# Moving the zero fill of the expert rows into the front, and a three-set ring in the edge count

## The chip, the cores and the metric

One Trainium2 chip, one of its cores. The time is device microseconds of one execution; the kernel before was timed three times.

## What is computed

One program chains four blocks on 1250 nodes with 512 features and 20000 edges sorted by receiver:

```python
x = x + graph_attention(layernorm(x), src, dst)      # softmax over edges, 8 heads
x = x + expert_ffn_top2(layernorm(x))                # 8 experts, capacity
x = x + tensor_product_messages(layernorm(x), edges) # MLP on edges, segment sum
x = x + expert_banks_top1(layernorm(x))              # two banks of 8 experts
```

The change touches the first one alone, and scratch memory that the second and the fourth use. The attention of the first block is done densely. Each pair (sender, receiver) gets the number of edges between them, and the logarithm of that number is added to the dense scores; a pair without an edge gets a very negative value. So three stages come first: the **front** (records of the edges are sorted into tiles of 128 edges, and queries, keys and values are computed), the **count** (the table of logarithms), and the attention itself.

## The kernel before, in words

Each stage is a block: its engines run their own programs, and all engines meet at its end, so a stage lasts as long as its slowest engine or queue.

**Front** (`front`, L137). The SP queue loads indices, attributes, x and the three weight matrices (L217), and later stores the queries to `q_dram` in eight transfers (L221), two for each of four groups of columns, each pair behind the evictions that fill the buffer QT (L219). ACT may refill QT for groups 2 and 3 only when the stores of groups 0 and 1 have landed. GpSimd (POOL) scatters the edge records: 157 indirect DMAs from `recs` to `rec_dram` (L266), one per column of 128 edges. They go in batches of 16, and batch b waits until all of batch b-2 have landed, so 16 to 32 are under way. VectorE (DVE) computes their positions, normalises x and computes tables: `low`, `turnI`, `spotI` and `endI` say for each tile of edges which block of receivers it belongs to, where its sums lie in PSUM and when a block is complete.

**Count** (`count_edges`, L561). The records come back as `recs_in`, in two parts. There are 176 tiles of 128 edges, worked in 44 sets of four. For a set DVE makes one `ohD` (L655: 4 one-hots of the receiver, 128 wide, all in one instruction) and four `ohS` (L659: the one-hot of half the sender's number, 625 columns used, WIDEN = 632 written). TensorE (PE) multiplies them: two matmuls a tile (512 and 113 columns, L677) add the counts into one of four regions of PSUM. ACT takes the logarithm of a finished block (L696) and clears its region (L701). The ring of one-hots holds CRING = 8 tiles, which is AHEAD = 2 sets: DVE waits before set g until PE has finished set g-2 (semaphore `counted`). PE reads the four PSUM offsets of a set from SBUF into registers with one TENSOR_LOAD (L670) ahead of the set; POOL reads a register for every set too (L620) and grants DVE the set when its region is free. The keys of the one-hots are computed by `keys` (L636 to L643) for the first 32 tiles at the start, and for the other 144 between sets 7 and 8.

In this stage the SP queue loads the records (L602) and the first queries (L545), and then calls `fill_zeros` (L606 to L609) for three arrays in DRAM: xin0 (4004 rows), xin_sp and xin_fq (2176 rows each), 512 floats a row, in pieces of 128 rows: 66 transfers. They stay zero until expert stages much later scatter rows into them. The stage's end waits for them.

At the end of its grants POOL splits the first tile of queries (L552, L554) for the attention.

Of the kernel before, what the change touches and what calls it, by code (L numbers as in the profile page):

```python
# [7 lines left out]
F16 = mybir.dt.float16  # L8
# [3 lines left out]
ALU = mybir.AluOpType  # L12
# [6 lines left out]
TILES = NODES // P  # L19
# [2 lines left out]


LANES, EPP = 128, 1
HALFB, BLOCKS, REGIONS, REGION, CRING = 64, 2 * TILES, 4, 1024, 8
EMAIN = EDGES // LANES
ETAIL = EDGES - EMAIN * LANES
ECOLS = EMAIN + 1
# [3 lines left out]
GROUPS = (EDGES + BLOCKS * GROUP) // GROUP  # L32
GROUPS += GROUPS % 2
ETILES = GROUPS * EPP
SLOTS = ETILES * LANES
assert GROUPS % 4 == 0 and CRING == 8
EHID = 64
ECHUNKS = -(-ETILES // 8)
REC = 16
# [16 lines left out]
BANKS = ("sp", "fq")  # L56
# [16 lines left out]
def gnn_moe_gnn_moe(nc, I, out):  # L73
# [17 lines left out]
    def sems_in(stack):  # L91

        def allocate(*names):
            handles = [nc.alloc_semaphore(name=fresh(n)) for n in names]
            stack.callback(finished.extend, handles)
            return handles
        return allocate
# [22 lines left out]
    with top:  # L120
        sb = tile_in(top)
# [15 lines left out]
        def front(KT, V, turnI, spotI, endI):  # L137

            with ExitStack() as st:
# [9 lines left out]
                done, moved, upper_moved, v_moved = sems_in(st)(  # L149
                    "product_done", "product_moved", "upper_moved", "values_moved")  # L150
                q_stored = sems_in(st)("queries_stored0", "queries_stored1")

                srcI, dstI = sb("srcI", [LANES, ECOLS], I32), sb("dstI", [LANES, ECOLS], I32)
                a4, a8 = sb("a4", [LANES, ECOLS, 4]), sb("a8", [LANES, ECOLS, 8])
# [42 lines left out]
                with nc.Block() as block:  # L197
                    @block.sync
                    def _(sp):
                        sp.dma_start(dstI[:, 0:EMAIN], main_part(I["dst"])).then_inc(dst_in, 16)  # L200
                        sp.wait_ge(blanked, 1)
                        sp.dma_start(dstI[0:ETAIL, EMAIN:], I["dst"][EMAIN * LANES:].rearrange("(p c) -> p c", c=1)).then_inc(dst_in, 16)
                        sp.dma_start(srcI[:, 0:EMAIN], main_part(I["src"])).then_inc(src_in, 16)
                        sp.dma_start(srcI[0:ETAIL, EMAIN:], I["src"][EMAIN * LANES:].rearrange("(p c) -> p c", c=1)).then_inc(src_in, 16)
                        sp.wait_ge(fill_ready, 1)
                        whole = rec_dram.rearrange("(p c) w -> p c w", p=LANES)
                        part = ETILES // FILLS
                        for f in range(FILLS):
                            sp.dma_start(whole[:, part * f:part * (f + 1), :], fill[:]).then_inc(filled, 16)
                        for tile, name in ((a4, "edge_attr_4"), (a8, "edge_attr_8")):  # L210
                            sp.dma_start(tile[:, 0:EMAIN, :], main_rows(I[name])).then_inc(attr_in, 16)
                            sp.dma_start(tile[0:ETAIL, EMAIN, :], I[name][EMAIN * LANES:, :]).then_inc(attr_in, 16)
                        x_rows = I["x"].rearrange("(t p) d -> p t d", p=P)
                        sp.dma_start(X[0:120], x_rows[0:120]).then_inc(x_in, 16)
                        sp.dma_start(X[120:P], x_rows[120:P]).then_inc(x_in, 16)
                        for i, name in enumerate(("L0_gnn_Wq", "L0_gnn_Wk", "L0_gnn_Wv")):
                            sp.dma_start(W[i][:], I[name].rearrange("(k p) n -> p k n", p=128)).then_inc(w_in[i], 16)  # L217
                        for j in range(KC):
                            sp.wait_ge(moved, (j + 1) * len(CHUNKS))  # L219
                            for half in range(2):  # L220
                                sp.dma_start(q_dram[:, 2 * j + half, :], QT[DK * half:DK * (half + 1), j % 2, :]).then_inc(q_stored[j % 2], 16)  # L221
                        for b in range(2):
                            sp.wait_ge(q_stored[b], 16 * KC)

                    @block.gpsimd
                    def _(pool):
# [334 lines left out]
        def count_edges(LA, stage, split, turnI, spotI, endI):  # L561

            HALFN = NODES // 2
            WIDEN = 632
            PARTS = [(0, 512), (512, HALFN - 512)]
            SET = 4
            AHEAD, SETS = CRING // SET, GROUPS // SET
            EARLY_ROUNDS = 4
            with ExitStack() as st:
# [1 line left out]
                RECS = sb("recs_in", [128, ETILES, REC])  # L571
                PARTS_OF_RECS = ((0, SET * AHEAD * EARLY_ROUNDS), (SET * AHEAD * EARLY_ROUNDS, ETILES))
                loaded = sems_in(st)("recs_loaded0", "recs_loaded1")
                numbered, cleared, steps, hot, counted, logged, evicted, zeroed, tick = sems_in(st)(
                    "nodes_numbered", "cleared", "steps", "one_hots_ready", "counted", "logged",
                    "evicted", "zeroed", "tick")
                (granted,) = sems_in(st)("region_granted")
                nodes16 = sb("nodes16", [128, WIDEN], F16)
                srcI, parityI = sb("srcI", [128, ETILES], I32), sb("parityI", [128, ETILES], I32)
                halfS, local, key16 = sb("halfS", [128, ETILES]), sb("local", [128, ETILES]), sb("key16", [128, GROUPS, EPP], F16)  # L580
                ohS, ohD = sb("ohS", [128, CRING, WIDEN], F16), sb("ohD", [128, CRING // SET, 2 * HALFB, SET], F16)
                keys_by_tile = sb("keys_by_tile", [128, 2 * HALFB, SET], F16)
                least = sb("least", [128, 1])
# [14 lines left out]
                with nc.Block() as block:  # L598
                    @block.sync
                    def _(sp):  # L600
                        for part, (c0, c1) in enumerate(PARTS_OF_RECS):
                            sp.dma_start(RECS[:, c0:c1, :], rec_dram.rearrange("(p c) w -> p c w", p=128)[:, c0:c1, :]  # L602
                                         ).then_inc(loaded[part], 16)
                        sp.wait_ge(loaded[1], 16)
                        stage(sp, 0)
                        zeros_in = fill_zeros(sp, xin0, zeroed)  # L606
                        for bank in BANKS:
                            zeros_in += fill_zeros(sp, xin1[bank], zeroed)
                        sp.wait_ge(zeroed, zeros_in)  # L609

                    @block.gpsimd
                    def _(pool):
# [14 lines left out]
                    @block.vector  # L627
                    def _(dve):
                        step = Chain(dve, steps)
                        nc.vector.memset(ps[:], 0.0).then_inc(cleared, 1)  # L630

                        def keys(part):
                            c0, c1 = PARTS_OF_RECS[part]
                            mine, groups_of = slice(c0, c1), slice(c0 // EPP, c1 // EPP)
                            dve.wait_ge(loaded[part], 16)
                            nc.vector.tensor_tensor(local[:, mine].rearrange("p (g t) -> p g t", t=EPP),  # L636
                                                    RECS[:, mine, 1].rearrange("p (g t) -> p g t", t=EPP),
                                                    low[:, groups_of].unsqueeze(2).to_broadcast([128, (c1 - c0) // EPP, EPP]), ALU.subtract)
                            step(nc.vector.tensor_copy(srcI[:, mine], RECS[:, mine, 0]))
                            nc.vector.tensor_scalar(parityI[:, mine], srcI[:, mine], 1, None, ALU.bitwise_and)  # L640
                            step(nc.vector.tensor_scalar(srcI[:, mine], srcI[:, mine], 1, None, ALU.arith_shift_right))
                            nc.vector.tensor_copy(halfS[:, mine], srcI[:, mine])
                            step(nc.vector.scalar_tensor_tensor(out=key16[:, groups_of, :].rearrange("p g t -> p (g t)"),  # L643
                                                                in0=parityI[:, mine], scalar=float(HALFB), in1=local[:, mine],
                                                                op0=ALU.mult, op1=ALU.add))

                        keys(0)
                        dve.wait_ge(numbered, 1)

                        def one_hots(g, k):  # L650
                            n = SET * g
                            dve.wait_ge(granted, g + 1)
                            dve.sem_inc(tick, 1)
                            dve.wait_ge(counted, n + SET)
                            nc.vector.tensor_tensor(ohD[:, k], keys_by_tile[:],  # L655
                                                    key16[:, bass.ds(n, SET), :].rearrange("p a t -> p (a t)")
                                                    .unsqueeze(1).to_broadcast([128, 2 * HALFB, SET]), ALU.is_equal)
                            for t in range(SET):
                                last = nc.vector.tensor_scalar(ohS[:, SET * k + t, :], nodes16[:], halfS[:, bass.ds(n + t, 1)],  # L659
                                                               None, ALU.is_equal)  # L660
                            last.then_inc(hot, 1)

                        groups(dve, one_hots, lambda: keys(1))
# [2109 lines left out]
```

## Time and profile before

| | us |
|---|---|
| median of 3 runs | 1884.42 |
| lowest, highest | 1881.56, 1887.0 |
| the profiled execution | 1887.7 |
| its span, first to last instruction | 1886.1 |

The profiled execution stands 3.3 us above the median of the runs, and 1.6 us of it lie outside its span. Mean granted TensorE clock 0.926. Over the span PE is busy 84%, DVE 51%, ACT 37%, POOL 30%. Such shares are averages over stages with different limits: what the change is worth has to be read in the front (0 to 233 us) and the count (233 to 325 us).

### The profile page before, as it was taken

What the parts mean: (1) busy time and instruction counts of PE and PEld (TensorE: products, weight loads), DVE (VectorE), ACT (ScalarE), POOL (GpSimd) and SP (SyncE); (2) the same over time, 40 slices, a digit from 0 to 9 for tenths busy, and PEclk for the clock granted to TensorE, in tenths of its full rate; (3) what the DMA queues carried; (4) which work ended last, traced back from release to release, by engine and by line L of the source; (5) the groups of instructions that cost most, each with busy time, mean ns of one, the idle gap of its engine ahead of it and who ended that gap; (6) DMA issues with size and microseconds to landing.
All of it is one profiled execution on the core that took longest, in us unless ns stands there. A gap on an engine that the chain in (4) does not pass through costs nothing. (4 is left out here: it accounts for less than half of the span.)

```text
span 1886.1 us, 31693 instructions
## 1 busy us (share of the span) xinstructions
PE 1592.0 (84%) x9860; PEld 1167.2 (62%) x9860; DVE 962.2 (51%) x1950; ACT 701.8 (37%) x1610; POOL 558.7 (30%) x638
## 2 busy tenths in 40 slices
PE   0993067999999797797999999848999999898994
PEld 0551034888888555555999999844555555655662
DVE  8320088677667287351000000068999999542233
ACT  1220045555555233443221111154555555431331
POOL 6777600110110032152000000045555555133133
PEclk6997589999999899798999999969999999998997
DMA  6200091110100510547556652075555555618985
GB/s 178 61 7 6 16 354 53 23 23 12 22 11 1 124 37 1 214 135 243 211 207 232 242 196 98 17 206 170 154 155 160 156 155 149 214 44 283 340 271 181
DMA packets 131144, 252.87 MB, mean 134 GB/s; under 512 B 35345, under 2 KB 52597, under 8 KB 126573
## 3 DMA queue, kind: packets, MB, share of 16 engines
q1 hardware_dynamic: 91692, 171.81, 27.5%
q0 software_dynamic: 39360, 79.86, 15.0%
q8 instruction: 55, 0.90, 0.2%
q14 instruction: 37, 0.30, 0.1%
HBM read 196.03 MB, written 55.52 MB: 133 GB/s over the span
## 5 line engine op out<-in xcount | busy, mean ns | idle before, releaser
L1998 PE MATMUL acc<-prod,ohy 128*64 128x256 f32 x1056 | 248.5, 385 | 7.8 <-DVE prod L2116 7.8
L2042 ACT ACTIVATE ohy<-oh,RECS 128x64 f32<-128x64 f32 x704 | 187.0, 336 | 151.4 <-PE acc L1998 151.4
L1998 PEld LDWEIGHTS acc<-prod,ohy 128*64 128x64 f32 x1056 | 138.3, 137 | 132.3 <-issue 70.6
L1975 POOL DMA_INDIRECT rows<-up_dram,idx x176 | 167.4, 951 | 143.0 <-DVE prod L2116 101.6
L266 POOL DMA_INDIRECT rec_dram<-recs,pos x157 | 160.2, 1021 | 59.6 <-issue 48.9
L2001 PE MATMUL acc<-prod,ohy 128*64 128x256 f32 x704 | 177.1, 394 | 0.0
L1752 DVE TENSOR_SCALAR FT<-y_ps,b2T 128x188 f32<-128x188 f32 x32 | 13.2, 414 | 319.8 <-PE y_ps L1701 319.8
L1689 PE MATMUL hid_ps<-FT,W 128*128 128x188 f32 x1024 | 168.0, 326 | 0.7 <-ACT FT L1726 0.7
L2116 DVE TENSOR_TENSOR prod<-w_ps,rows 128x768 f32<-128x768 f32 x176 | 166.3, 945 | 0.0
L1689 PEld LDWEIGHTS hid_ps<-FT,W 128*128 128x128 f32 x1024 | 165.6, 192 | 0.9 <-issue 0.9
L1701 PE MATMUL y_ps<-hid,W 128*128 128x188 f32 x1024 | 164.5, 323 | 0.0
L1701 PEld LDWEIGHTS y_ps<-hid,W 128*128 128x128 f32 x1024 | 162.9, 190 | 0.0
L842 DVE CUSTOM_DVE_ANT_0 S<-score_ps,LA 125x1250 f32<-125x1250 f32 x80 | 116.7, 1459 | 77.4 <-PE score_ps L758 76.5
L903 ACT ACTIVATE S<-S,mx 125x1250 f32<-125x1250 f32 x80 | 107.3, 1341 | 116.2 <-DVE mx L847 116.2
L677 PE MATMUL ps<-ohS,ohD 128*128 128x512 f16 x352 | 60.3, 320 | 106.1 <-DVE ohS L659 100.1
L2061 DVE TENSOR_TENSOR MSG<-MSG,acc 128x512 f32 x178 | 120.7, 678 | 3.5 <-PE acc L1998 0.5
L677 PEld LDWEIGHTS ps<-ohS,ohD 128*128 128x128 f16 x352 | 38.7, 117 | 128.3 <-issue 123.1
L758 PE MATMUL score_ps<-KT,QS 128*125 128x512 f32 (+1 forms) x480 | 113.1, 371 | 4.0 <-PEq L598 2.1
L767 PE MATMUL turn_ps<-ident,S 125*125 125x125 f32 x800 | 108.4, 283 | 1.2 <-ACT PT L908 1.1
L776 PE MATMUL out_ps<-PT,V 125*64 125x125 f32 x1600 | 103.0, 274 | 1.5
L1637 POOL DMA_DIRECT2D yout<-ye x7 | 11.8, 1692 | 307.4 <-DVE ye L1757 307.4
L767 PEld LDWEIGHTS turn_ps<-ident,S 125*125 125x125 f32 x800 | 94.4, 190 | 12.9 <-issue 11.2
(380 smaller groups left out, 2632.4 us busy)
## 6 DMA issues: line engine op xcount, KB each, us to landing
W<-in_L_ffn_w SPq DMA_DIRECT2D x16, 4096.0 KB, 16.7
bankW_sp<-in_L_ffn_W_sp SPq DMA_DIRECT2D x2, 4096.0 KB, 23.8
xin<-zeros SPq DMA_DIRECT2D x31, 256.0 KB
h_dram<-h3e SPq DMA_DIRECT2D x22, 256.0 KB, 4.5
h<-h_dram SPq DMA_DIRECT2D x22, 256.0 KB, 2.7
QF<-q_dram SPq DMA_DIRECT2D x20, 250.0 KB, 4.3
xin_sp<-zeros SPq DMA_DIRECT2D x17, 256.0 KB
xin_fq<-zeros SPq DMA_DIRECT2D x17, 256.0 KB
```

Source lines behind the costliest of these rows:

```text
L266: pool.indirect_dma_start(out=rec_dram, out_offset=bass.IndirectOffsetOnAxis(ap=pos[0:rows_of, c:c + 1], axis=0), in_=recs[0:rows_of, c, : ...
L758: last = nc.tensor.matmul(score_ps[:P, c0:c0 + cn], QS[par][:, part, h, 0:P], KT[:, h, c0:c0 + cn], start=part == 0, stop=part == 1)
L767: last = nc.tensor.transpose(turn_ps[:P, 128 * s:128 * s + P], S[:, h % 2, P * s:P * (s + 1)], ident[:P, :P])
L842: nc.vector.tensor_tensor_reduce(out=S[:, h % 2, :], in0=score_ps[:P, 0:NODES], in1=LA[:, 2 * pairs - 2 + par, :], scale=1.0, scalar=-3e38 ...
L1689: last = nc.tensor.matmul(hid_ps[:, m % 4, 0:ROWS0], W1[b][:, k, 128 * m:128 * (m + 1)], xT[:, k, :], start=k == 0, stop=k == KC - 1)
L1701: last = nc.tensor.matmul(y_ps[:, d % 2, 0:ROWS0], W2[b][:, m, 128 * d:128 * (d + 1)], hid[:, m, :], start=m == 0, stop=m == MC0 - 1)
L1975: pool.indirect_dma_start(out=rows[:, t, :], out_offset=None, in_=up_dram, in_offset=bass.IndirectOffsetOnAxis(ap=idx[:, par, t:t + 1], ax ...
L1998: upper = lambda m: nc.tensor.matmul(acc[0:HALFB, bank, :].rearrange("p (b c) -> p b c", c=MUL)[:, m:4:3 - m, :], ohs[:, 1 + m, :], pr[:, ...
L2001: lower = lambda q: nc.tensor.matmul(acc[HALFB:128, bank, 256 * q:256 * (q + 1)], ohs[:, 0, :], pr[:, 0:3:2, :] if q == 0 else pr[:, 3:5, ...
L2042: last = nc.scalar.activation(ohy[:, t % OHY, i, :], oh[:, par, t, :], ACT.Copy, scale=RECS[:, bass.ds(BATCH * g + t, 1), 4 + i])
L2061: nc.vector.tensor_tensor(sums, sums, acc[:, bank, :], ALU.add).then_inc(taken, 1)
L2116: nc.vector.tensor_tensor(pr[:, 2:8, :].rearrange("p (a m) c -> p a m c", a=2), w[:, 2:4, :].unsqueeze(2).to_broadcast([128, 2, 3, MUL]), ...
```

## The change

The 66 transfers of zeros go to the SP program of the front: behind the loads of the weights, ahead of the stores of the queries; the front's end waits for them in place of the count's. The ring of one-hots grows from 8 to 12 tiles (AHEAD 2 to 3). With it the first part of the records becomes 48 tiles, not 32 (the second 128, not 144), the loops over sets are unrolled three times, not twice, and two sets stand behind the loop. `endI` follows CRING. To make room, WIDEN becomes 626, and `halfS` and `local` go: both are written in place over columns 0 and 1 of the records (16 floats apart), and `ohS` reads its scalar there.

```diff
-HALFB, BLOCKS, REGIONS, REGION, CRING = 64, 2 * TILES, 4, 1024, 8
+HALFB, BLOCKS, REGIONS, REGION, CRING = 64, 2 * TILES, 4, 1024, 12
...
                             sp.dma_start(W[i][:], I[name].rearrange("(k p) n -> p k n", p=128)).then_inc(w_in[i], 16)
+                        sp.wait_ge(consts, 1)
+                        zeros_in = fill_zeros(sp, xin0, zeroed)
+                        for bank in BANKS:
+                            zeros_in += fill_zeros(sp, xin1[bank], zeroed)
                         for j in range(KC):
                             sp.wait_ge(moved, (j + 1) * len(CHUNKS))
...
                         for b in range(2):
                             sp.wait_ge(q_stored[b], 16 * KC)
+                        sp.wait_ge(zeroed, zeros_in)
...
-            WIDEN = 632
+            WIDEN = 626
...
-                halfS, local, key16 = sb("halfS", [128, ETILES]), sb("local", [128, ETILES]), sb("key16", [128, GROUPS, EPP], F16)
+                key16 = sb("key16", [128, GROUPS, EPP], F16)
...
                         sp.wait_ge(loaded[1], 16)
                         stage(sp, 0)
-                        zeros_in = fill_zeros(sp, xin0, zeroed)
-                        for bank in BANKS:
-                            zeros_in += fill_zeros(sp, xin1[bank], zeroed)
-                        sp.wait_ge(zeroed, zeros_in)
...
-                            nc.vector.tensor_tensor(local[:, mine].rearrange("p (g t) -> p g t", t=EPP),
-                                                    RECS[:, mine, 1].rearrange("p (g t) -> p g t", t=EPP),
-                                                    low[:, groups_of].unsqueeze(2).to_broadcast([128, (c1 - c0) // EPP, EPP]), ALU.subtract)
+                            nc.vector.tensor_tensor(RECS[:, mine, 1], RECS[:, mine, 1], low[:, groups_of], ALU.subtract)
...
-                            nc.vector.tensor_copy(halfS[:, mine], srcI[:, mine])
+                            nc.vector.tensor_copy(RECS[:, mine, 0], srcI[:, mine])
...
-                                last = nc.vector.tensor_scalar(ohS[:, SET * k + t, :], nodes16[:], halfS[:, bass.ds(n + t, 1)],
+                                last = nc.vector.tensor_scalar(ohS[:, SET * k + t, :], nodes16[:], RECS[:, bass.ds(n + t, 1), 0],
```

The helper that it calls:

```python
        def fill_zeros(sp, target, zeroed):
            starts = range(0, target.shape[0], 128)
            for r in starts:
                m = min(128, target.shape[0] - r)
                sp.dma_start(target[r:r + m, :], zeros[:m, :]).then_inc(zeroed, 16)
            return 16 * len(starts)
```

## Rows read from the trace of the kernel before

**Rows 1.** Table of stretches: front after PE's start, its tail, the flood, the quiet.

```profile
core 0: us, PE busy (x) PEld busy (x) DVE busy (x) ACT busy (x) POOL busy (x), PEclk, DMA share, GB/s
60.00:150.00 90.00, 90.00 (x246) 46.22 (x245) 16.32 (x33) 22.23 (x43) 68.46 (x71) 1.00 0.16 35
150.00:228.00 78.00, 6.68 (x16) 2.63 (x14) 0.00 (x0) 1.64 (x3) 58.02 (x61) 0.57 0.04 6
264.00:286.00 22.00, 14.59 (x94) 10.07 (x92) 18.58 (x59) 13.54 (x18) 0.00 (x0) 1.00 1.02 378
289.00:308.00 19.00, 15.22 (x99) 10.58 (x98) 18.87 (x61) 13.52 (x17) 0.00 (x0) 1.00 0.00 1
```

**Rows 2.** Timeline of the SP queue: start, length of issue, line, transfer.

```profile
15.09 4.68 SPq L217 DMA_DIRECT2D Wqkv<-in_L_gnn_Wv  x1
64.02 26.28 SPq L221 DMA_DIRECT2D q_dram<-QT  x8
240.57 22.44 SPq L1536 DMA_DIRECT2D xin<-zeros  x32
274.49 12.34 SPq L1536 DMA_DIRECT2D xin_fq<-zeros  x17
```

**Rows 3.** The SP queue's own wait at the end of the count.

```profile
SPq L598 <- DMA xin_fq<-zeros: 3.0, 1, 3.0
```

**Rows 4.** POOL's scatter L266: the whole front, then 60 to 100 us.

```profile
L266 POOL DMA_INDIRECT rec_dram<-recs,pos x157: 869/967/4703, 18.5 to 226.8; - x157
L266 POOL DMA_INDIRECT rec_dram<-recs,pos x32: 963/967/970, 60.2 to 99.6; - x32
```

**Rows 5.** A stretch in which query stores load the DMA engines during the scatter.

```profile
82.00:84.00 2.00, 2.00 (x6) 0.88 (x5) 0.00 (x0) 0.15 (x1) 1.70 (x2) 1.00 0.95 197
```

**Rows 6.** POOL's ten scatters L2570 late in the kernel, while bank weights load.

```profile
DMA to landing us min/median/max: 8.0/9.3/11.6
```

**Rows 7.** TENSOR_LOAD L670 (ns min/median/max): 264 to 286 us, then 289 to 312.

```profile
L670 PEldq TENSOR_LOAD <-spotI x12: 625/930/1077, 264.5 to 285.8; - x12
L670 PEldq TENSOR_LOAD <-spotI x14: 328/332/335, 289.4 to 309.7; - x14
```

**Rows 8.** Waits from 215 to 345 us: us in total, times, longest.

```profile
DVE ohD L655 <- PE ps L677: 8.4, 17, 1.4
```

**Rows 9.** Timeline of DVE in the count: first set, keys, quiet sets, collision, last set.

```profile
238.88 0.42 DVE L655 TENSOR_TENSOR ohD<-keys_by_tile,key 128x512 f16<-128x512 f16 x1 [0.54 <-POOLq L622]
239.23 1.26 DVE L659 TENSOR_SCALAR ohS<-nodes,halfS 128x632 f16<-128x632 f16 x4
240.40 0.41 DVE L655 TENSOR_TENSOR ohD<-keys_by_tile,key 128x512 f16<-128x512 f16 x1
...
253.58 0.39 DVE L636 TENSOR_TENSOR local<-recs_in,low 128x144 f32<-128x144 f32 x1
...
255.57 0.42 DVE L655 TENSOR_TENSOR ohD<-keys_by_tile,key 128x512 f16<-128x512 f16 x1 [0.52 <-DVE key L643]
...
289.86 0.42 DVE L655 TENSOR_TENSOR ohD<-keys_by_tile,key 128x512 f16<-128x512 f16 x1
...
307.11 0.42 DVE L655 TENSOR_TENSOR ohD<-keys_by_tile,key 128x512 f16<-128x512 f16 x1
...
312.84 0.41 DVE L655 TENSOR_TENSOR ohD<-keys_by_tile,key 128x512 f16<-128x512 f16 x1
...
320.11 0.43 DVE L655 TENSOR_TENSOR ohD<-keys_by_tile,key 128x512 f16<-128x512 f16 x1
```

**Rows 10.** Timeline of PE and POOL at the collision.

```profile
309.68 2.18 POOL L554 TENSOR_TENSOR QS<-QF,QS 128x1000 fp32r<-128x1000 f32 x1
...
313.06 5.18 PE L677 MATMUL ps<-ohS,ohD 128*128 128x512 f16 x24 [2.97 <-DVE ohS L659]
```

**Rows 11.** The shortest DVE TENSOR_SCALAR, one column: busy us, mean ns.

```profile
L886 DVE TENSOR_SCALAR has<-mx 125x1 f32<-125x1 f32 x10 | 1.0, 102 | 0.0
```

**Rows 12.** Timeline of DVE in the front: the twenty 157-column one-hots.

```profile
4.55 3.19 DVE L286 TENSOR_SCALAR ge<-dst 128x157 f16<-128x157 f16 x20
```

More of the change, by code:

```diff
@@ L35 @@
 SLOTS = ETILES * LANES
-assert GROUPS % 4 == 0 and CRING == 8
+assert GROUPS % 4 == 0 and CRING % 4 == 0
 EHID = 64
@@ L151, in front @@
                 q_stored = sems_in(st)("queries_stored0", "queries_stored1")
+                (zeroed,) = sems_in(st)("rows_zeroed")
                 srcI, dstI = sb("srcI", [LANES, ECOLS], I32), sb("dstI", [LANES, ECOLS], I32)
@@ L573, in count_edges @@
                 loaded = sems_in(st)("recs_loaded0", "recs_loaded1")
-                numbered, cleared, steps, hot, counted, logged, evicted, zeroed, tick = sems_in(st)(
+                numbered, cleared, steps, hot, counted, logged, evicted, tick = sems_in(st)(
                     "nodes_numbered", "cleared", "steps", "one_hots_ready", "counted", "logged",
-                    "evicted", "zeroed", "tick")
+                    "evicted", "tick")
                 (granted,) = sems_in(st)("region_granted")
@@ L641, in keys @@
                             step(nc.vector.tensor_scalar(srcI[:, mine], srcI[:, mine], 1, None, ALU.arith_shift_right))
-                            nc.vector.tensor_copy(halfS[:, mine], srcI[:, mine])
+                            nc.vector.tensor_copy(RECS[:, mine, 0], srcI[:, mine])
                             step(nc.vector.scalar_tensor_tensor(out=key16[:, groups_of, :].rearrange("p g t -> p (g t)"),
-                                                                in0=parityI[:, mine], scalar=float(HALFB), in1=local[:, mine],
+                                                                in0=parityI[:, mine], scalar=float(HALFB), in1=RECS[:, mine, 1],
                                                                 op0=ALU.mult, op1=ALU.add))
```

## The prediction, on record before the changed kernel ran

> **What bounds the kernel now.** I read the table of stretches first, then the SP queue's timeline, then the groups and waits inside the count.
>
> The front ends with POOL, not with PE, DVE or the DMA engines. From 150 to 228 us PE is busy 6.7 of 78 us and DVE not at all, while POOL works through its scatters at a DMA share of 0.04 [rows 1]. The 157 scatters start between 18.5 and 226.8 us, one every 1.27 us in steady state: (226.8 - 60.2) / 131 for the last ones [rows 4]. So the DMA engines have room there, and whatever else is put in the front costs nothing as long as the scatters keep their pace.
>
> The count has two faces. From 289 to 308 us DVE is busy 18.87 of 19 us and bounds the stage: 11 sets between the `ohD` at 289.86 and the one at 307.11, which is 1.568 us a set [rows 1, 9]. From 264 to 286 us, while zeros fill the DMA engines (share 1.02, 378 GB/s), DVE is busy only 18.58 of 22 us and waits for PE, though PE is busy just 14.59 us [rows 1]. What holds PE is its register read: the TENSOR_LOAD ahead of each set takes 930 ns in the flood (median) and 332 ns without it [rows 7]. The matmuls of a set last 1.24 us (14.59 us for 94, eight a set [rows 1]), and the load can't overlap most of them, so a set takes PE 22 / 11.75 = 1.87 us there, above DVE's 1.57. DVE's waits for PE add up to 8.4 us [rows 8]. The zeros are issued from 240.57 to 286.83 us (46.3 us for 66 transfers) and the last lands some 3 us later [rows 2, 3]; the stage goes on past 320, so their own end holds nobody.
>
> **The change, part by part.** The sum is made on DVE's stream of sets, since its last `ohD` (320.11) sets the end of the count in both kernels.
>
> Before: first `ohD` 238.88, last 320.11, that is 81.2 us for 43 steps [rows 9].
>
> After, with no wait for PE: 43 x 1.568 = 67.4 us. To this come the second part of the keys, 255.57 - 253.58 = 2.0 us, and the collision with POOL's split of the queries: from 307.11 to 312.84 DVE needed 5.73 us for two sets that otherwise take 3.14, so 2.6 us [rows 9, 10]. The split follows POOL's last grants and so stays a few sets ahead of the end; I keep the 2.6. The sum is 72.0 us, 9.2 less than before. The wait row gives nearly the same from the other side: 8.4 us [rows 8].
>
> That all of the waits go, not only those of the flood, rests on the ring. Three PE sets at the low clock took 5.18 us after the collision, 1.73 a set against DVE's 1.57 [rows 10]; with three sets in the ring DVE runs through such a stretch. The ring alone would do little against the flood, because there PE's rate, not its latency, is short.
>
> Small terms. The loop over sets is unrolled thrice. The step from 238.88 to 240.40 holds no turn of the loop and takes 1.52 us, the mean of quiet steps is 1.568 with a turn in every second, so a turn costs about 0.1 us [rows 9]; 22 turns become about 15, -0.6 us (bounds 0 and -0.7). WIDEN 632 to 626: 6 columns at 0.28 ns (worked out below) by 176 are -0.3 us. The in-place keys write every sixteenth float: two copies, each bounded by the strided subtraction's 0.39 us [rows 9]; I take +0.3 us. Part 0 of the records grows from 256 to 384 KB and loads while DVE clears PSUM; if that cover fell short it would be by less than 1 us. The second part of the keys now comes after set 11, at the same cost. DVE's extra run-ahead costs no PSUM, since grants are as before; POOL's and ACT's register reads get shorter too, off the path. Together -0.6.
>
> In the front SP is free for zeros from 19.8 us [rows 2]; they share the engines with x and the weights, which are ahead of them in the same queue, and need their 46 us after that, so they flow until about 80 us. Past them are moved the stores of the queries, first issued at 64.02: they come up to 15 us late, and ACT's refill of QT a few us late. PE and ACT have that slack many times over: PE's work ends before 160 us, the stage near 230. The scatters: during the flood some 35 of them are issued. The nearest rows say that their issue does not care. From 60 to 100 us, while the query stores run, 32 scatters take 963/967/970 ns, and in 82 to 84 us the share is 0.95 [rows 4, 5]. Their landing may be late: under weight loads ten scatters landed after 8 to 11.6 us [rows 6]; but a batch waits for records issued at least 16 x 1.27 = 20 us earlier, so this is hidden, with 9 us to spare. Cost of the move: 0, bounds 0 and +14 to +25 (the rival below). A gain has no ground there, since the scatters run at their pace already.
>
> The Trainium skill has a rule against this: "DMA: Bandwidth & Descriptors", queues, rings and completion order, says each DMA engine round-robins between queue rows and drains a whole packet, of some 9 to 17 descriptors, before it switches. By it each scatter would stand behind packets of zeros; no row here shows packets in such a mix. At worst this lengthens the landings above.
>
> Sum: -9.2 - 0.6 = -9.8 us; the wait row would make it -9.0. I take **-9.5**. On the profiled execution: span 1886.1 to 1876.6, time 1887.7 to 1878.2. The median of the runs stands 3.3 lower: 1884.4 to **1874.9**.
>
> **The rivals.**
>
> *The scatter slows (slower side).* Place: L266 during the flood, 35 to 80 us. POOL also reads its positions from SBUF, as PE reads its offsets, and the flood made that read longer by 0.6 us [rows 7]. If each scatter took 0.6 us more, a pace of 1.87 would lose 45 x (1 - 1.27/1.87) = 14 us; if its 0.967 us grew by the same factor, 930/332 = 2.8, the pace would be 3.0 and the loss 26 us. Against -9.5 this gives +5 to +16: 1889 to 1901, most likely 1893. It decides from a loss of 9.5 us, a mean DMA_INDIRECT above 1.31 us in the flood. For it: nothing here shows a scatter against writes of zeros from SBUF at 380 GB/s. Against it: 970 ns at most under the stores [rows 4], which also go from SBUF to DRAM. Chance 8%.
>
> *The narrow one-hot loses its rate (slower side).* Place: L659, 176 times. 626 columns split in two halves of 313, an odd number, and the second half no longer begins on a 4-byte boundary. The 632-column form comes every (240.40 - 239.23) / 4 = 0.293 us [rows 9]. The 157-column one of the front takes 3.19 / 20 = 0.160 [rows 12]; the difference is 0.28 ns a column, with a fixed 0.116 us, near the 0.102 of a one-column instruction [rows 11]. So 157, odd in length and in its halves' start, runs at the rate of 632. If 626 did run at half that rate, it would cost 626 x 0.28 = 0.175 us more by 176, 31 us, for a net +21: 1906. Chance 4%. The Trainium skill speaks on both sides: "VectorE: DVE Perf Modes", mode 2×_1P, asks for 4-byte alignment; "Vector Engine (DVE) Microarchitecture Reference", section 5.1, says that alignment makes no difference, and the 157-column one-hots [rows 12] agree with the latter.
>
> *PE's clock takes part of it back.* With the waits gone PE still idles 0.3 us a set, and it starts the stage cold. At the low level three sets took 5.18 us [rows 10]. If about half of the 44 sets ran so, PE would bound them at 1.73 to 1.95, and the gain would lose 22 x 0.16 to 0.38 = 3.5 to 8 us: a gain of 1.5 to 6, 1878.5 to 1883. Against it: from 289 to 308 us, at just this load, the clock stayed at 1.00 [rows 1]. Chance 16%.
>
> *More than the sum.* DVE, three sets ahead, loses less in the collision, or the split slides behind the last set: 2.6 us more, and PE's cold start is absorbed too: -12 to -13, 1872. Chance 10%.
>
> **How the numbers follow.** The forecast (gain 7 to 11.5, 1873 to 1877.5) has 62%. About 0.3%, 5.6 us, is what a measurement of this kernel can tell from no change. Faster by more: 62 + 10 and a part of the clock's case, 76%. Within: the rest of the clock's case and the gentler end of the scatter's, 14%. Slower: 10%. The range reaches from the "more" case to the clock's case, with a us for the spread of medians: 1870 to 1881.5.
>
> **What would show it.** TENSOR_LOAD L670 near 330 ns throughout; DVE's wait for PE under 1.5 us; count from first to last `ohD` near 71.5 us; `ohS` at 0.29 us a piece; scatters in 35 to 80 us at 0.97 and the last one starting at 226.8 as before; zeros issued from about 20 to 77 us. Wrong it would be if the front's last scatter moves, if `ohS` takes 0.47, or if PE runs at 0.5 clock in the middle of the count.

## The result, and the profile after

| | before | changed |
|---|---|---|
| median of 6 runs, us | 1884.07 | 1871.24 |
| lowest, highest | 1881.56, 1887.0 | 1868.04, 1875.17 |
| ratio, 95% interval | | 0.9936 [0.9917, 0.9954] |
| span of the profiled execution | 1886.1 | 1873.4 |

The change gained 12.8 us in the medians, 12.7 in the spans; 9.5 were forecast. A second series (e0 below) gave 0.9947 [0.9927, 0.9966].

**The count.** First and last `ohD`, and the quiet and flooded stretches of before [rows 1, 9], now (timeline of DVE, then the table of stretches):

```profile
239.54 0.42 DVE L655 TENSOR_TENSOR ohD<-keys_by_tile,key 128x512 f16<-128x512 f16 x1 [0.54 <-DVE key L643]
...
241.05 0.42 DVE L655 TENSOR_TENSOR ohD<-keys_by_tile,key 128x512 f16<-128x512 f16 x1
...
299.13 0.41 DVE L655 TENSOR_TENSOR ohD<-keys_by_tile,key 128x512 f16<-128x512 f16 x1
299.47 3.94 DVE L659 TENSOR_SCALAR ohS<-nodes,recs_in 128x626 f16<-128x626 f16 x4
303.33 0.41 DVE L655 TENSOR_TENSOR ohD<-keys_by_tile,key 128x512 f16<-128x512 f16 x1
...
309.36 0.41 DVE L655 TENSOR_TENSOR ohD<-keys_by_tile,key 128x512 f16<-128x512 f16 x1
```

```profile
core 0: us, PE busy (x) PEld busy (x) DVE busy (x) ACT busy (x) POOL busy (x), PEclk, DMA share, GB/s
264.00:286.00 22.00, 18.70 (x117) 12.63 (x116) 22.00 (x74) 17.56 (x23) 0.00 (x0) 1.00 0.00 1
```

From the first one-hot to the last it takes 69.8 us, not 81.2, so 11.4 us are gained. DVE is busy 22.00 of 22 us, and nearly every step from one `ohD` to the next is 1.51 us. Its waits for PE (8.4 us [rows 8]) are gone from the table of waits; what is left of idle time before `ohD` is 1.1 us behind its own keys. The steps that are longer are two at PE's cold start (1.71 and 1.57 us), the one with the second keys and the one at the collision. The collision with POOL's split still costs 4.20 - 1.51 = 2.7 us. The register reads of PE stay short, but for the first one (531 ns at 238.1 us), over all 44 sets (min/median/max ns, against 625/930/1077 in [rows 7]):

```profile
L670 PEldq TENSOR_LOAD <-spotI x44: 327/331/531, 238.1 to 310.6; - x44
```

**The front.** SP's timeline, POOL's scatter over the whole front and from 20 to 80 us, its landing from 20 to 80 us, and a stretch of the table:

```profile
19.29 35.31 SPq L1536 DMA_DIRECT2D xin<-zeros  x32
54.64 12.86 SPq L1536 DMA_DIRECT2D xin_sp<-zeros  x17
67.54 13.31 SPq L1536 DMA_DIRECT2D xin_fq<-zeros  x17
80.90 10.74 SPq L226 DMA_DIRECT2D q_dram<-QT  x8
```

```profile
L272 POOL DMA_INDIRECT rec_dram<-recs,pos x157: 873/968/4706, 18.9 to 227.4; - x157
L272 POOL DMA_INDIRECT rec_dram<-recs,pos x42: 963/970/4706, 18.9 to 79.6; - x42
DMA to landing us min/median/max: 3.0/4.8/10.2
```

```profile
64.00:80.00 16.00, 16.00 (x46) 8.29 (x45) 0.00 (x0) 1.92 (x4) 12.03 (x14) 1.00 0.98 341
```

The zeros are issued until 80.9 us, the queries' stores begin 17 us late, DMA share is 0.98, and the scatters keep 970 ns. The last one starts at 227.4 (226.8 before, and 226.8 again in e0). Of the 12.7 us in the span the later start of the count takes back 0.65, the count gives 11.4, and 2.0 lie behind the attention's start, in stages that the change does not touch; the six runs of the changed kernel alone spread over 7.1 us, so these 2.0 us are not shown to come from the change.

### The profile page after: what moved, and what is told of

It reads as the page before. It is cut to its first block and busy times, and to the rows that moved or that the text cites. A ratio compares the mean times of both kernels' runs of the same rounds, so it can differ in the third digit from the quotient of the medians.

```text
span 1873.4 us, 31644 instructions
## 1 busy us (share of the span) xinstructions
PE 1594.3 (85%) x9860; PEld 1167.9 (62%) x9860; DVE 959.7 (51%) x1950; ACT 701.4 (37%) x1610; POOL 559.6 (30%) x638
## 5 line engine op out<-in xcount | busy, mean ns | idle before, releaser
L1637 POOL DMA_DIRECT2D yout<-ye x7 | 11.8, 1691 | 307.5 <-DVE ye L1757 307.5
```

## Experiments

The experiments ran on three chips. e0 to e3 ran on the first, where the kernel before takes 1882.75 us (29 runs); e4 to e7 on a second, where it takes 1973.33 us (34 runs); e8 to e11 on a third, where it takes 1976.8 us (23 runs). Each is compared with the kernel before on its own chip. The changed kernel as it stands ran on neither of the slower chips.

**e1: the move of the zeros alone.** Of the diff, only the `fill_zeros` lines; CRING 8, WIDEN 632, `halfS` and `local` stay.

> The kernel before with only the zeros moved into the front: ring of two sets, 632 columns, halfS and local as before. Theory A (the flood made PE's register read long, and that read held PE in the count): TENSOR_LOAD at 330 ns throughout, DVE steps of 1.52 and 1.61 us in turn (mean 1.57) from the start, some waits left at PE's cold start and at its low clock. First to last ohD about 73 us against 81.2 before and 69.8 after; time 7 to 9 us below the kernel before. Rival (the ring is what did it, the flood's end helps little): first to last ohD above 78 us, under 4 us gained.

The ratio is 0.9970 [0.9953, 0.9986], a gain of 5 us. From first to last `ohD` it takes 75.0 us, which is 6.3 of the 11.4 gained. TENSOR_LOAD is at 328/332/529 ns (min/median/max). The reading holds, but both numbers miss: 73 us and a gain of 7 to 9 us were expected. This is the quiet pace with two sets in the ring:

```profile
286.02 0.42 DVE L657 TENSOR_TENSOR ohD<-keys_by_tile,key 128x512 f16<-128x512 f16 x1
286.36 1.26 DVE L661 TENSOR_SCALAR ohS<-nodes,halfS 128x632 f16<-128x632 f16 x4
287.64 0.43 DVE L657 TENSOR_TENSOR ohD<-keys_by_tile,key 128x512 f16<-128x512 f16 x1
287.98 1.26 DVE L661 TENSOR_SCALAR ohS<-nodes,halfS 128x632 f16<-128x632 f16 x4
289.16 0.42 DVE L657 TENSOR_TENSOR ohD<-keys_by_tile,key 128x512 f16<-128x512 f16 x1
```

In the long step (1.62 us) the next `ohD` starts only when the four `ohS` have ended (287.62); in the short one (1.52) it starts 0.08 us before they end (289.24). Of the 5.1 us that e1 has more than the changed kernel, some 2.7 are this alternation (a mean of 1.58 us against 1.51 over 38 steps), 1.4 PE's cold start (steps of 2.63 and 2.09 us, against 1.71 and 1.57) and 1.1 the step behind the collision (2.63 us), where DVE waits for PE.

**e2: the ring alone.** The changed kernel with the `fill_zeros` lines back in the count.

> The changed kernel with the zeros back in the count: ring of three sets, 626 columns. Theory A: in the flood PE is bound by its read and a deeper ring can't raise a rate, so some 23 sets go at 1.85 to 2.0 us; outside it sets go at 1.507. First to last ohD 76 to 79 us, time 2 to 5 us below the kernel before. Rival (the ring hides the long read, since DVE runs three sets ahead): under 72 us, 9 us or more gained.

The ratio is 0.9977 [0.9963, 0.9992], a gain of 4 us. First to last `ohD` is 75.75 us, just under the expected 76 to 79, and 5.5 of the 11.4 gained. The two parts nearly add: 6.3 + 5.5 = 11.8. In the flood PE still reads long, and late in it the sets go at 2.0 to 2.2 us. But DVE does seven of its first eight steps at 1.50 to 1.52 us, and six more at 1.50 to 1.54 behind the second keys, during which PE catches up: the third set absorbs PE's lag for a while. Outside the flood the ring ends the alternation and the wait behind the collision. The first line is PE's read in the flood, the second its waits from 215 to 345 us for nothing that the profile shows ("issue"):

```profile
L668 PEldq TENSOR_LOAD <-spotI x24: 463/816/1050, 241.6 to 285.4; - x24
PE ps L675 <- issue: 9.0, 15, 0.8
```

The kernel before has 6.0 us of such waits, e1 and the changed kernel have no such row. The matmuls themselves are not longer in the flood (14.59 us for 94, 0.155 each, against 15.22 for 99, 0.154 [rows 1]), so it is between the sets that PE loses time.

```profile
264.00:286.00 22.00, 14.25 (x90) 9.56 (x88) 18.49 (x60) 14.01 (x18) 0.00 (x0) 1.00 0.99 368
```

**e3: what the alternation is.** e1 with four sets in a turn of the loop, and half as many turns (one of the two loops is shown):

```diff
-                            for k in range(AHEAD):
-                                body(AHEAD * r + k, k)
+                            for k in range(2 * AHEAD):
+                                body(2 * AHEAD * r + k, k % AHEAD)
```

> As e1_zeros_only, but the loops over sets hold four sets a turn in place of two (the ring stays at two sets, slots k % 2). Separates two readings of the alternation 1.52 and 1.61 us, whose end brought more than I had summed. If it is the loop's turn on DVE's sequencer, only every fourth step is 1.61: mean 1.54, first to last ohD about 1 us shorter than in e1. If it is the way back from PE (DVE may not begin set g before PE has finished set g-2), the steps alternate as in e1 or all stand near 1.57, and the time is that of e1.

```profile
286.87 0.42 DVE L657 TENSOR_TENSOR ohD<-keys_by_tile,key 128x512 f16<-128x512 f16 x1
288.49 0.43 DVE L657 TENSOR_TENSOR ohD<-keys_by_tile,key 128x512 f16<-128x512 f16 x1
290.00 0.42 DVE L657 TENSOR_TENSOR ohD<-keys_by_tile,key 128x512 f16<-128x512 f16 x1
291.62 0.42 DVE L657 TENSOR_TENSOR ohD<-keys_by_tile,key 128x512 f16<-128x512 f16 x1
```

The steps are 1.62, 1.51 and 1.62 us with half the turns, so it is not the loop. The ratio is 0.9970 [0.9955, 0.9985] as in e1, and first to last `ohD` is 76.0 us; the one more than in e1 is a step of 2.64 us behind the keys. What is left is the way back from PE: with two sets DVE waits for set g-2 and gets its word just too late. That the alternation ends with three sets (e2, the changed kernel) fits; why it comes every second time no run shows.

**e0: the changed kernel again,** beside e1 to e3.

> The changed kernel once more, on the chip of these three, to compare them with. As before: 12 to 13 us below the kernel before, first to last ohD 69.8 us, DVE's wait for PE near 0.

The median is 1872.41 us, 10.3 below the kernel before, where 12 to 13 were expected. First to last `ohD` is 69.8 us, and there is no wait for PE.

**e8: the kernel before, on the third chip.**

> The kernel before, for its trace on the chip of these four. If the chip is one on which it takes 1973 us, as for e4 to e7: the front is ended by PE, near 312 us as in e7 (whose front is that of the kernel before), and the changed kernel's front (320 to 322 us in e4 to e6) is 8 us longer than it. If it is one on which it takes 1883 us: count of 81 us from 239, as before.

One run took 1974.11 us. PE in the front, POOL's scatter, a stretch of the table, and PE's register read in the flood of the count:

```profile
122.70 1.01 PE L410 MATMUL ps<-FT,Wqkv 128*128 128x512 f32 x1 [1.79 <-issue]
125.50 1.01 PE L410 MATMUL ps<-FT,Wqkv 128*128 128x512 f32 x1 [1.79 <-issue]
```

```profile
L266 POOL DMA_INDIRECT rec_dram<-recs,pos x157: 869/967/4705, 18.7 to 227.0; - x157
60.00:120.00 60.00, 24.86 (x52) 11.62 (x52) 2.29 (x10) 2.96 (x5) 45.47 (x48) 0.64 0.04 7
L670 PEldq TENSOR_LOAD <-spotI x23: 611/867/1027, 322.1 to 365.6; - x23
```

POOL is as on the first chip, but PE gets a matmul every 2.80 us between about 100 and 240 us, though it waits for nothing that the profile shows ("issue"). The granted clock from 120 to 228 us is 0.50. The front ends with PE near 312 us: the records are loaded from 313.6, where the first chip does so from 233.0. e7, on the second chip, shows the same. What spaces PE's instructions there is open. The count is the same, 80.8 us.

**e4: zeros written twice in the front.** `fill_zeros` is called for the three arrays a second time, when the first zeros have landed.

> The changed kernel with the 66 transfers of zeros issued twice in the front, one after the other. Theory A: the front is set by POOL's scatters and has room for far more traffic, so their number doubled (the flood then lasts to about 125 us) changes nothing: DMA_INDIRECT at 970 ns, last scatter within 1 us of 227.4, time within 2 us of the changed kernel. Rival (each scatter or the queries' stores behind the flood do pay a little, and the 0.5 us later end of the front after the change is that): last scatter later by 1 us or more, or PE's end of the front near POOL's.

```profile
L276 POOL DMA_INDIRECT rec_dram<-recs,pos x157: 876/971/4701, 19.2 to 228.2; - x157
60.00:120.00 60.00, 3.20 (x12) 2.12 (x12) 4.23 (x14) 3.54 (x6) 45.69 (x48) 0.50 0.62 217
```

The scatters do not care even about twice the zeros, issued until 186 us: they take 971 ns, and the last starts at 228.2, where the single dose in e5 has 228.3. That settles the scatter's rival. But PE, which bounds the front on these chips, did 12 matmuls from 60 to 120 us. With the single dose it did 12 to 15 (e5, e6, e10), and in fronts without zeros 40 to 56 (e7, e8, e9, e11). It makes good most of it later. The records are loaded from 320.5 to 322.1 us in the four kernels with zeros in the front, and from 312.8 (e7), 313.6 (e8), 316.6 (e9) and 317.7 (e11) in those without: the move costs between 3 and 9 us there, and the second dose no more. In the changed kernel's own profile PE lost nothing: 247 matmuls from 60 to 150 us, against 246 before [rows 1]. The time is 1970.5 us, the ratio 0.9982 [0.9966, 0.9998].

**e5 and e10: the split behind the last one-hot.**

```diff
                         groups(pool, grant)
+                        pool.wait_ge(hot, SETS)
                         split(pool, 0, 0)
```

> The changed kernel, but POOL splits the first queries only after DVE's last one-hot (a wait for hot = 44 ahead of the split). Theory: the 4.2 us step of the collision becomes 1.5, so DVE's stream is 2.7 us shorter (67.1), PE's clock does not fall near the end, but the split (3.3 to 3.8 us) now ends the stage, some 3.5 us behind the last one-hot where PE's last matmul stood 3.0 behind it with the collision: the attention begins 1.5 to 3 us earlier. Rival: the split becomes the end of the stage and eats it all, attention within 0.7 us of the changed kernel.

> e5 once more. From the first one-hot to the attention's first matmul 72.9 us, where the changed kernel has 75.0: 2 us gained on the changed kernel. On a chip of 1883 us that makes 12 to 15 us below the kernel before; on one of 1973 us 3 to 6.

First to last `ohD` takes 67.3 and 67.2 us, with no long step. From the first `ohD` to the attention's first matmul it takes 72.9 and 72.7 us; the changed kernel has 75.0 (239.54 to 314.51), and e4 and e6, on the chip of e5, have 75.2 and 75.4. So 2 us or a little more of the collision are saved, and the split's own end takes the rest back. The ratios to the kernel before are 0.9975 [0.9958, 0.9992] and 0.9964 [0.9947, 0.9981], on chips where the front takes some of it back.

**e6: an odd width.** `WIDEN = 625`.

> The changed kernel with 625 columns in a one-hot: an odd row, so every second one-hot begins off a 4-byte boundary. Theory (neither an odd count nor alignment takes the rate away, as the 157-column one-hots suggested): ohS unchanged at 0.29 to 0.30 us a piece, step 1.507, time as the changed kernel. Rival (alignment or evenness matters, and 626 was just even enough): ohS about 0.17 us longer, step near 2.2, count 30 us longer.

```profile
L659 DVE TENSOR_SCALAR ohS<-nodes,recs_in 128x625 f16<-128x625 f16 x176 | 58.0, 394 | 0.0
```

The mean of 626 columns after the change is 392 ns, of 632 before 388, and the steps stay at 1.51 us. Neither evenness nor the boundary costs a rate. The ratio is 0.9989 [0.9971, 1.0007].

**e7 and e9: zeros in the count, but copied from DRAM.** e2, with the first piece written from SBUF and waited for, and the other 65 copied from it (the loop over the pieces is left out):

```diff
+                        sp.dma_start(xin0[0:128, :], zeros[:, :]).then_inc(zeroed, 16)
+                        sp.wait_ge(zeroed, 16)
...
+                            sp.dma_start(target[r:r + m, :], xin0[0:m, :]).then_inc(zeroed, 16)
```

> As e2_ring_only, but only the first piece of zeros comes from SBUF; the other 65 are copied from it, DRAM to DRAM, in the count. Tells what lengthens the engines' register reads. If it is the traffic's reading of SBUF: TENSOR_LOAD stays near 330 ns and the count goes at 1.507 a set, first to last ohD near 70 us. If it is busy DMA engines or DRAM in general: TENSOR_LOAD 600 ns or more, 75 us or more.

> e7 once more. On a chip where the kernel before takes 1883 us: front as before (last scatter 226.8), first to last ohD 69.6 to 70 us, so 10 to 12 us below the kernel before, level with the changed kernel. On one where it takes 1973 us: 7 to 10 us below the kernel before, 4 to 8 below the changed kernel.

PE's read during the copies, and a stretch of the table in e7:

```profile
L672 PEldq TENSOR_LOAD <-spotI x28: 327/331/334, 324.6 to 367.2; - x28
350.00:360.00 10.00, 8.75 (x56) 5.93 (x55) 10.00 (x34) 7.88 (x11) 0.00 (x0) 1.00 1.02 328
```

The DMA engines are as full as in the flood (share 1.02), and the read takes 331 ns, not 816. On one and the same chip the kernel before has 867 ns (e8) and the copies have 331 (e9). So it was not busy DMA engines that held PE, but traffic whose source is SBUF. The one piece that e9 does write from SBUF, in flight until 328 us, has a read of 808 ns beside it (at 325.2 us). Two things stay open: the copies move somewhat less (293 to 328 GB/s, against 368 to 391), and traffic that only writes SBUF was not tried by itself. First to last `ohD` is 69.6 us in e7, with the zeros still in the stage. The ratios are 0.9955 [0.9939, 0.9970] and 0.9948 [0.9921, 0.9974]: 8 and 13 us in the medians, more than any kernel with the zeros in the front reaches on these chips, though the intervals overlap with those of e5 and e10. In e9 no step is long (66.8 us): POOL's copy began at 381.46 and took 10.50 us, so this time DVE kept POOL out, not POOL DVE.

**e11: both.**

> Both: ring of three sets, zeros in the count copied DRAM to DRAM, queries split after the last one-hot. If the two gains add: on a chip of 1883 us 13 to 15 us below the kernel before, on one of 1973 us 10 to 12 below it, the fastest of all kernels tried on either.

The time is 1965.61 us, the ratio 0.9946 [0.9926, 0.9966], 11 us below. From the first `ohD` to the attention it takes 72.7 us, against 74.9 in e7 and 72.2 in e9, whose profiled execution happened to have no long step. The time is level with e9 (1963.33), so a gain of the late split over e9 is not shown, and e11 is not the fastest of all kernels, though that was expected. None of e7, e9 and e11 ran on the first chip, so whether the copies beat the changed kernel there is open.

## Why the prediction came out as it did

- **Direction and mechanism were right.** The front ends with POOL's scatters and hid the zeros; the flood lengthened PE's read, and with it the count's sets (e1, e7).
- **The cost of the move, 0:** right where the kernel before takes some 1883 us, within about 1 us. There the last scatter starts at 226.8 to 227.9 us in the four profiles with zeros in the front (the changed kernel, e0, e1, e3), and at 226.8 and 226.7 in the two without (before, e2). The grounds were slack of PE and ACT; on the slower chips PE has none, and the same move costs 3 to 9 us. The prediction had one chip's trace.
- **The size was short, by 3.2 us in the spans and by 0.8 in the second series.** In the count it was short by 1.6 us: 71.4 forecast, 69.8 measured. The mis-sized term is the step: "43 x 1.568 = 67.4" took the quiet pace for DVE's own, because the waits table showed nothing. It was still the ring's pace. With three sets the step measured 1.507, so 64.8, which is 2.6 us less. The -0.6 for turns of the loop was the same 0.1 us with a wrong cause (e3), and has to be left out. Then 64.8 + 2.0 for the keys + 2.7 for the collision + 0.3 for PE's cold start = 69.8, as measured. The rest of the 3.2 us is 0.3 of rounding in the forecast and the 2.0 behind the attention's start, less 0.65 for the count's later start. So part of the median's distance from the forecast is chance.
- **"The ring alone would do little against the flood" was wrong in its size.** It raises no rate in the flood, as e2's 2.0 to 2.2 us show, but it bridges PE's slow stretches and ends the alternation: 5.5 us alone.
- **Arbitration.** The Trainium skill's rule ("DMA: Bandwidth & Descriptors", queues, rings and completion order) is consistent with what was seen: scatters from 20 to 80 us land after 4.8 us (median), against 2.1 for the same stretch of before. No view shows packets, so the rule itself is not shown. The longest landing, 10.2 us, is none of the zeros' doing, for the kernel before has one of 10.0 there; it is within the 20 that a batch has.
- **Scatter rival:** it fell with the changed kernel's own 970 ns and with e4 (971 ns).
- **Narrow one-hot:** it fell with e6. The Trainium skill's section 5.1 of "Vector Engine (DVE) Microarchitecture Reference", by which alignment makes no difference, agrees with 394 ns for 625 columns.
- **PE's clock:** it fell once more at the end (granted clock 0.50 from 305 to 307 us; six sets took 8.84 us from 303.55), and the ring absorbed it. The rival's 1.73 us a set came from a stretch at mixed levels (0.75, 0.50 and 0.84 between 313 and 318.2 us), so it was not the price of the low level. At 0.50, from 241.7 us on, PE loads the weights of a tile every 0.52 us, some 2.1 us a set.
- **More than the sum:** the nearest in size, but hardly for its reason. The collision stayed at 2.7 us, and that PE's cold start is absorbed (all but 0.3 us) was already in the sum, which had no wait for PE.

## What to carry to other kernels

Work that nobody waits for is not free where it runs: look at what the register reads of the engines' sequencers take beside it, and try another source (here DRAM in place of SBUF) or a stage that has no such reads on its path. A pace that alternates while the waits table is empty can be a ring one set too short, as it was here. A stage with slack on one chip may be another chip's bound, so a move into it should be timed on more than one.

## What was not expected of the hardware

- A transfer's source decides whether it disturbs: SBUF to DRAM at share 0.99 to 1.02 lengthened TENSOR_LOAD from 330 to 816 (e2), 867 (e8) or 930 ns (before); DRAM to DRAM at the same share left it at 331 (e7, e9).
- When DVE's one-hots and POOL's copy meet, either can lose: in the changed kernel DVE's four `ohS` took 3.94 us instead of 1.26; in e9 POOL's copy took 10.50 us instead of 1.03, and DVE's steps stayed at 1.51. What decides it is open.
- Chips differ by 90 us on one program: on two of the three, PE's instructions in the front came 1.40 us apart (a weight load and a matmul, 2.80), and with zeros in flight PE did 12 to 15 matmuls from 60 to 120 us, where it did 40 to 56 without.
